# Reordered attention queues, a scale factor computed early, and a square root moved from GpSimd to ScalarE, in an attention, convolution and whitening kernel

## What is computed

```python
# L0: attention, C/8 = 8 query and key channels, 32 value channels
q, k, v = Wq @ x + bq, Wk @ x + bk, Wv @ x + bv
x = gamma * (Wo @ (v @ softmax(q.T @ k).T) + bo) + x
# L1: the same without Wo and gamma, 64 value channels
x = x + v @ softmax(q.T @ k).T
# L2: two rounds of batch norm, relu, 3x3 convolution with weights E*sign(w), E = mean|w|
out = conv3x3(relu(bn(x, g0, b0)), E0*sign(w0))
x = conv3x3(relu(bn(out, g1, b1)), E1*sign(w1)) + x
# L3: whitening: 16 groups of 4 channels, over all images and pixels
cov = xc @ xc.T / N;  U = cholesky(cov + eps*I).T;  out = weight @ solve(U, xc) + bias
```

## Time and profile before

| | us |
|---|---|
| median of 3 runs (lowest, highest) | 69.20 (69.17, 69.22) |
| the profiled execution, its own time | 69.05 |
| span of that execution in the profile | 67.3 |
| PE busy / DVE busy / ACT busy / POOL busy | 57.7 / 48.0 / 42.5 / 20.0 |

### The profile page before, as it was taken

How to read it: one execution, slowest core, us unless ns; L and a number is a source line. 1 busy time by engine, 2 the same in 40 slices (tenths; PEclk the granted TensorE clock), 3 DMA queues, 4 the chain that set the end, 5 groups by cost and what they waited for, 6 DMA issues and landing times. The chain is left out here.

```text
span 67.3 us, 2133 instructions
## 1 busy us (share of the span) xinstructions
PE 57.7 (86%) x795; PEld 36.7 (54%) x795; DVE 48.0 (71%) x133; ACT 42.5 (63%) x137; POOL 20.0 (30%) x58
## 2 busy tenths in 40 slices
PE   5994898889899989958998989999499999999910
PEld 3323433655465627432553758698385997855500
DVE  0079899595949899994946775988949978575530
ACT  0711098999997699789998663930028564167630
POOL 5000955530554608680303040301303050045000
PEclk9999999999999999999999999999999999999999
DMA  0998930000000000000000000000000000000044
GB/s 0 254 245 205 370 151 0 0 0 10 0 0 5 0 0 0 0 19 0 0 0 0 0 0 10 0 0 10 0 0 0 10 0 0 10 0 0 0 166 146
DMA packets 2457, 2.71 MB, mean 40 GB/s; under 512 B 400, under 2 KB 2064, under 8 KB 2448
## 3 DMA queue, kind: packets, MB, share of 16 engines
q1 hardware_dynamic: 2160, 2.39, 11.5%
q10 hardware_dynamic: 288, 0.20, 0.9%
HBM read 2.06 MB, written 0.52 MB: 38 GB/s over the span
## 5 line engine op out<-in xcount | busy, mean ns | idle before, releaser
L507 ACT ACTIVATE bank<-bank,negmax 128x256 f32<-128x256 f32 x32 | 14.5, 457 | 1.7 <-DVE negmax L1054 1.7
L683 PE MATMUL bank<-const-bfloat16-1.0 128*64 128x512 bf16 x82 | 11.5, 418 | 0.8 <-PEq L1362 0.8
L1054 DVE TENSOR_REDUCE negmax<-bank 128x2 f32<-128x512 f32 x16 | 10.5, 685 | 1.9 <-PE bank L742 1.8
L527 ACT ACTIVATE probs<-bank 128x512 f32<-128x512 f32 x16 | 8.8, 602 | 1.1 <-PE bank L766 1.1
L805 PE MATMUL bank<-probs,vt 128*64 128x256 f32 x64 | 8.5, 386 | 0.3 <-DVE cut L1064 0.3
L910 PE MATMUL bank<-hi,taps 64*64 64x225 f16 (+2 forms) x144 | 6.9, 267 | 0.1
L683 PEld LDWEIGHTS bank<-const-bfloat16-1.0 128*64 128x64 bf16 x82 | 4.7, 117 | 4.2 <-issue 1.6
L507 ACT ACTIVATION_READ_ACCUMULATOR bank<-bank,negmax 128x1 f32 x32 | 6.9, 216 | 0.0
L910 PE MATMUL bank<-lo,taps 64*64 64x225 f16 (+2 forms) x144 | 6.9, 266 | 0.0
L360 POOL TENSOR_TENSOR cut<-cut 64x256 f32<-64x256 f32 x7 | 4.3, 610 | 8.3 <-DVE cut L1064 5.3
L910 PEld LDWEIGHTS bank<-hi,taps 64*64 64x64 bf16 x144 | 5.8, 107 | 0.9 <-issue 0.4
(11 more groups left out here) (134 smaller groups left out, 103.3 us busy)
## 6 DMA issues: line engine op xcount, KB each, us to landing
cw<-conv_w SPq DMA_DIRECT2D x2, 288.0 KB, 4.2
x<-x_in SPq DMA_DIRECT2D x4, 128.0 KB, 2.6
out<-res SPq DMA_DIRECT2D x4, 128.0 KB, 1.8
kst<-consts SPq DMA_DIRECT2D x1, 428.0 KB, 4.9
aw<-attn_w ACTq DMA_DIRECT2D x1, 128.0 KB, 2.5
aw<-attn_w SPq DMA_DIRECT2D x1, 128.0 KB, 3.0
half<-select SPq DMA_DIRECT2D x1, 96.0 KB, 2.7
kst<-consts SPq DMA_DIRECT2D x1, 64.5 KB, 3.4
```

What stands on the lines that cost most here:

```text
L507: nc.scalar.activation(part, part, ACT.Exp, bias=negmax[:, i % 2, n:n + 1], accum_out=total[:, i % 2, n:n + 1]).then_inc(total_out, 1)
L527: nc.scalar.activation(probs[:, i % 2, g], pb_t[g][:].rearrange("p (t n) -> p t n", t=CH), ACT.Exp).then_inc(exp_out, 1)
L683: mm(bank[lanes(h)], filler[:, lanes(h)], filled, start=True, stop=True)
L1054: ve.tensor_reduce(negmax[:, i % 2, g * CH:(g + 1) * CH], pb_s[(2 * i + g) % 3][:].rearrange("p (t n) -> p t n", t=CH), AX.X, ALU.max, neg ...
```

## The change

It has six edits. (a) On PE, `project(3)` goes behind `scores(0)` and `scores_t(0)`. (b) On PE, the block `values(3)`, `scores(4)`, `scores_t(3)`, `shifts_to_rows(3)`, `mix(2)` becomes `scores(4)`, `shifts_to_rows(3)`, `scores_t(3)`, `mix(2)`, `values(3)`; on DVE `values_out(3)` goes behind the maxima of step 4 and `add_shortcut(2)`. (c) On DVE, `weight_sum(0)` goes behind `maxima(6, 1)`. (d) On DVE, `power_of_two(1)` goes from the first convolution to attention, behind `statistics(0)`. (e) The second root is computed by ACT as exp(-0.5 ln) instead of by POOL, which keeps the first and the third. (f) The fourth output piece has PSUM banks of its own, and PE's two waits ahead of it go.

```diff
-        pb_out = [[banks[n] for n in ns] for ns in ((6, 7), (4, 5), (2, 0), (6, 7))]
+        pb_out = [[banks[n] for n in ns] for ns in ((6, 7), (4, 5), (2, 0), (1, 3))]
...
-                pool.wait_ge(root_out, j + 1)
+                pool.wait_ge(root_out, 1 if j == 0 else 2)
             pool.wait_ge(a_out, 1)
             power(0)
-            for j in range(1, Q - 1):
-                pool.wait_ge(pivot_out, j)
-                power(j)
+            pool.wait_ge(pivot_out, 2)
+            power(2)
...
-            for n in range(2):
-                act.wait_ge(root_out, n + 1)
-                if n:
-                    act.wait_ge(hot_out, 1)
-                nc.scalar.activation(hot01[n][:], hot01[0][:] if n else hot, ACT.Identity,
-                                     scale=roots[:, n:n + 1]).then_inc(hot_out, 1)
+            act.wait_ge(pivot_out, 1)
+            nc.scalar.activation(lnp[:, 0:1], tt[:, 1, 1:2], ACT.Ln).then_inc(lnp_out, 1)
+            act.wait_ge(lnp_out, 1)
+            nc.scalar.activation(roots[:, 1:2], lnp[:, 0:1], ACT.Exp,
+                                 scale=kst[:, K_EXPO + 1:K_EXPO + 2]).then_inc(root_act, 1)
+            act.wait_ge(root_out, 1)
+            nc.scalar.activation(hot01[0][:], hot, ACT.Identity, scale=roots[:, 0:1]).then_inc(hot_out, 1)
+            act.wait_ge(root_act, 1)
+            act.wait_ge(hot_out, 1)
+            nc.scalar.activation(hot01[1][:], hot01[0][:], ACT.Identity, scale=roots[:, 1:2]).then_inc(hot_out, 1)
...
             project(2)
-            project(3)
             scores(0)
             scores_t(0)
+            project(3)
...
             project(5)
-            values(3, 3)
             scores(4)
+            shifts_to_rows(3, 3)
             scores_t(3)
-            shifts_to_rows(3, 4)
             mix(2)
+            values(3, 4)
             replicate(5)
...
-                if n == 3:
-                    pe.wait_ge(res_act, 1)
-                    pe.wait_ge(res_dve, 1)
...
-            values_out(3)
             maxima(4, 0)
             maxima(4, 1)
             add_shortcut(2)
+            values_out(3)
...
-            weight_sum(0)
             maxima(6, 0)
             values_out(5)
             maxima(6, 1)
+            weight_sum(0)
...
             statistics(0)
+            power_of_two(1)
             values_out(6)
...
                     later_inputs(0, 3)
-                    power_of_two(1)
                     conv0_statistics(0)
```

More of the change, by code:

```diff
@@ L187, in build @@
         roots = sb("roots", [P, Q - 1])
-        lnp = sb("lnp", [P, 1])
+        lnp = sb("lnp", [P, 2])
         hot01 = [sb(f"hot01{n}", [P, Q]) for n in range(2)]
@@ L259, in build @@
         pivot_out, root_out, piv_out, a_out = sem("pivot_out"), sem("root_out"), sem("piv_out"), sem("a_out")
+        root_act = sem("root_act")
         lnp_out = sem("lnp_out")
@@ L641, in _ @@
                                      bias=dmean[:]).then_inc(zc_out, 1)
-            for n in range(2):
-                act.wait_ge(root_out, n + 1)
-                if n:
-                    act.wait_ge(hot_out, 1)
-                nc.scalar.activation(hot01[n][:], hot01[0][:] if n else hot, ACT.Identity,
-                                     scale=roots[:, n:n + 1]).then_inc(hot_out, 1)
+            act.wait_ge(pivot_out, 1)
[8 more added lines that the diff above has]
+            nc.scalar.activation(hot01[1][:], hot01[0][:], ACT.Identity, scale=roots[:, 1:2]).then_inc(hot_out, 1)
             act.wait_ge(pivot_out, Q - 1)
-            nc.scalar.activation(lnp[:], tt[:, Q - 1, Q - 1:Q], ACT.Ln).then_inc(lnp_out, 1)
-            act.wait_ge(lnp_out, 1)
-            nc.scalar.activation(piv[:], lnp[:], ACT.Exp, scale=kst[:, K_EXPO + Q - 1:K_EXPO + Q]).then_inc(piv_out, 1)
+            nc.scalar.activation(lnp[:, 1:2], tt[:, Q - 1, Q - 1:Q], ACT.Ln).then_inc(lnp_out, 1)
+            act.wait_ge(lnp_out, 2)
+            nc.scalar.activation(piv[:], lnp[:, 1:2], ACT.Exp, scale=kst[:, K_EXPO + Q - 1:K_EXPO + Q]).then_inc(piv_out, 1)
             for q in range(2, PAIRS):
@@ L1296, in _ @@
             dve.wait_ge(hot_out, 2)
-            dve.wait_ge(root_out, Q - 1)
+            dve.wait_ge(root_out, 2)
             step(ve.scalar_tensor_tensor(prod[:], tt[:, :, Q:2 * Q].rearrange("p i r -> p r i"), roots[:, Q - 2:Q - 1],
```

## The result

| | before | after |
|---|---|---|
| median (lowest), us | 69.21 (69.17) | 68.73 (68.59) |
| ratio of times, 95% interval | | 0.993 (0.991 to 0.9949) |
| the profiled execution, its own time / span | 69.05 / 67.3 | 68.74 / 66.9 |
| PE / DVE / ACT / POOL busy | 57.7 / 48.0 / 42.5 / 20.0 | 58.1 / 48.4 / 43.1 / 20.0 |

The interval, taken of 69.21, is a gain of 0.35 to 0.62. The forecast of 68.7 came within 0.03 of the median, but the terms behind it did not all come so near: one gained more than I said, one lost where I had put nothing.

The account below looks back on a forecast made before the run. A chain of waits over keep-warm matmuls, second convolution and DVE work between convolutions was taken to bound it; 0.19 + 0 + 0 + 0.28 + 0.02 + 0 = 0.49 off 69.05 gives 68.56, median 68.7, range 68.05 to 69.0.

Parts of the forecast that it names:

- (a): Start, PE: first scores 0.27 earlier, second scores behind the keep-warm matmuls 0.19 earlier; 0.19 gained, bounds 0 to 0.27.
- (b): Attention, PE and DVE: ACT's idle time moves behind its totals and is not won; 0, bounds 0.1 lost to 0.5 gained.
- (c): DVE at step 6: the later weight sum runs mostly in a wait for the replication; 0, bounds 0 to 0.05 lost.
- (d): Power of two moved into attention: 0.78 gained between the convolutions, less 0.5 for DVE held by POOL; net 0.28.
- The cover in attention: DVE's 0.86 wait for the values at 35.31 hides the added 1.0 of power of two: cost 0, 0.4 to spare.
- the hold: First convolution: POOL's product of the second taps slows DVE's two low parts by 0.5, bounds 0 to 0.75.
- The first rival: DVE is not held by POOL's product: 0.78 kept, total gain 0.99, a median run takes 68.2; chance 0.35.
- (e) and (f): End: earlier final weights hidden by keep-warm matmuls, 0.02 gained; fourth output piece's own banks hidden by transfer spacing, 0.
- The third rival: DVE in attention has no room for the added 1.0, values copy late: a median run takes 69.4; chance 0.06.

Follow-up runs that it names:

- the change without (c): The changed kernel with the weight sum back in its old place, ahead of the maxima of step 6: 68.42, ratio 0.9881.
- (c) alone: The kernel before with only the weight sum moved behind the maxima of step 6: 70.69; in its profiled execution TensorE's granted clock fell to 1.2 GHz.
- late taps: The changed kernel with one added wait, so POOL starts the second taps' product only after DVE's last low part: 68.47, ratio 0.9902.
- the other form of the square: The changed kernel with the one-column square as a tensor_scalar with one tile input instead of a tensor_tensor: 68.47, ratio 0.989.
- the change with the early weight sum: The changed kernel with the weight sum behind the maxima of step 3 instead of those of step 6: 68.54, ratio 0.9933.

## Why the prediction came out as it did

**(a), 0.19: near in size, in part by luck.** The first half of the chain held: first scores behind the copy, maxima with them, and 0.23 at the exponentials. The second half did not. I had named the keep-warm group as the limit and put 0.19 on the second scores behind it. They gained 0.09, and nothing that follows was held by them: POOL's shifts and the exponentials of step 0 need the first scores, and those carried 0.23 on. So the limit was the wrong one. The group itself stayed where I said (1.84 behind the first `qk` copy), but the scores behind it come 1.19 after its start and not 1.08, since the five pairs at 0.215 are followed by 0.11 more. And the claim that "every later step waits for these engines and for no load that would stay where it is" missed that PE has places of its own: 0.09 is gone by step 5. That 0.19 lies between the 0.23 won and the 0.13 kept is chance.

One reading of the start was wrong too, though no term hangs on it: "The granted clock is full throughout". Up to 2.9 the keep-warm pairs of the kernel before start 0.43 apart, and in the group at 8.28 0.215 apart.

**(b), 0: right**, with its reason. ACT's idle time went behind its totals, and the replication came 0.13 later against step 2's exponentials, where I had counted 0.11. Alone it costs 0.08, inside the 0.1 of the bound; beside (a) it costs nothing more.

**(c), 0: the mis-sized term, 0.14 to 0.21 lost against a bound of 0.05.** Two steps failed. I let all that stands behind the weight sum move up when the sum is taken away. But the copy of the values waits for PE and stays (29.33, 29.38 before), the time won turns into 0.19 and 0.29 of idle time ahead of the maxima and ahead of the copy, and the second maxima start at 29.82 and not earlier than 29.71. From 29.71 the sum would be through at 29.71 + 0.61 + 0.66 = 30.98, 0.10 behind the copy's old start; the 0.11 by which the maxima are late make it 31.09. The other step was that nobody behind that copy needs it in time. In the change without (c) and in (c) alone the delay arrives whole at the exponentials of step 6 and at `mv`.

**(d), 0.28: right in sign and mechanism, 0.51 in size.** The cover in attention held: no wait of PE for the values copy, cost 0. On the hold I had the right event and the wrong victim. I let the product stop the low parts for 0.5. In fact the low parts stopped the product (0.75 became 1.30), and the product then stopped the one-column square for 0.27 (0.43 against 0.16). The late taps give back all of it and lose 0.07 to another hold, the other form of the square gives 0.22 back. With a hold of 0.27 my own sum reads 0.78 - 0.27 = 0.51, which is what was measured: the 0.78 was right. The first rival, no hold, is the case of the late taps but for that 0.07; the hold between the two cases was real, and half of what I took.

**(e) and (f), 0.02: right**, 0 measured, with the cover that was named. Taking six keep-warm matmuls away uncovers 0.36.

**The sum.** Predicted 0.19 + 0 + 0 + 0.28 + 0.02 = 0.49. By the marks of the profile: attention 0.02 (the distance from the first `qk` to the first `mv` is 34.88 before and 34.85 after, where the 0.16 of (a) and (b) and the loss of (c) nearly cancel), between the convolutions 0.51, behind them 0: 0.53. By the times 0.48. That I came within 0.03 is luck, two errors that cancel: 0.17 too much for (a) to (c) together and 0.23 too little for (d). The third rival, no room on DVE in attention, was refuted for the power of two at its place; but the part of it that says DVE has less room than it seems is just what (c) ran into, some 4 us earlier.

**The chain of waits misleads in one place.** In the profile after it runs through the first convolution on PE, and PE would be called the bound from 43.20 to 48.19. Yet freeing DVE's square alone took 0.22 off that stretch. The convolution has the same 144 matmuls in both, over 5.03 in the one and 4.82 in the other. Where PE stands still for DVE's next quarter, two starts lie 0.28 and 0.31 apart (at 44.98 and 45.81) instead of 0.12 or less, but each record is 0.26 long and covers nearly all of it. So the wait looks like work.

## What to carry to other kernels

When a filler instruction moves behind a group of others, ask of each one in the group whether it can move up at all; if one waits for another engine, the room that was left there is lost and the filler pays in its new place. Put a filler where an idle time of its own length stands ahead of an instruction that waits for something else. When a wide POOL instruction lands beside DVE work, list the DVE instructions by form, not by size: here the one-column products of two inputs in SBUF that began in its middle were held to its end. A form with one tile input took most of the cost away. A later start of POOL only moved the hold to another product, so ask of that one too who waits for what stands behind it.

## What the hardware showed that I had not expected

**Holds go both ways.** POOL's product (0.75 alone) took 1.30 in both traces shown and in two more, in which the low parts ran in its first half, although its record starts 0.02 before theirs (43.38 against 43.40, 43.20 against 43.22). Later DVE instructions with two inputs were held to POOL's end to within 0.01 (44.68 and 44.68; 48.20 and 48.19; the same in three more traces). The rule of the Trainium skill cited in the prediction (SBUF — State Buffer, SBUF: two separate sides) says that the one who starts first keeps the port pair for the whole instruction. The runs agree with it for the square, the late product and the square in another form; for the low parts they agree only if POOL takes hold of the port later than its record starts. One-column roots on POOL (59.44, 0.56 long) still didn't hold a DVE instruction with two inputs (59.55, 0.24), and that stays unexplained.

**A lag behind a keep-warm group.** Matmuls behind it start 0.11 to 0.15 later than its pitch gives: 1.19 against 5 x 0.215 = 1.08 at the start, and 62.34 - 58.96 = 3.38 against 15 x 0.215 = 3.23 at the end.

**A copy and the maxima behind it.** In the change the maxima start 0.49 behind the start of a copy of 0.42 (29.33 to 29.82), in the kernel before 0.33 (29.38 to 29.71), and in the change with the early weight sum 0.34 behind a copy that also had waited for PE (30.11 to 30.45). The copy's wait is thus not the reason; what is, I did not find.
